# Attention block over 16 images on one core: all engines' programs written out, VectorE's work between two images in another order, and a new start and end

## The reference

```python
xn = group_norm(x)                      # 32 groups, no scale or bias
q, k, v = split(xn.T @ qkv_w.T + qkv_b)
q, k = relu(q), relu(k + pos_enc)       # 8 heads of 32 channels
z   = 1 / (q . sum_tokens(k) + 1e-6)    # per token and head
out = (q @ (k.T @ v)) * z               # linear attention, per head
y   = x + out @ proj_w.T + proj_b
```

## Time and profile before

| what | value |
|---|---|
| median of 3 runs | 2903.65 us (2902.27 to 2904.47) |
| the profiled execution's own time | 2910.53 us |
| its span | 2908.7 us |
| mean granted TensorE clock | 0.993 |
| busy: PE, DVE, ACT, POOL | 94%, 73%, 60%, 53% of the span |

### The profile page before, as it was taken

The page is one execution under the profiler, slowest core; times in us unless marked ns, Lnnn a source line. Parts: engine busy times, 40 slices in busy tenths (PEclk is TensorE's granted clock), DMA queues, the critical chain, the costliest instruction groups (busy, mean ns, idle before and its releaser), DMA issues.

```text
span 2908.7 us, 50163 instructions
## 1 busy us (share of the span) xinstructions
PE 2727.0 (94%) x16232; PEld 2303.3 (79%) x16232; DVE 2115.0 (73%) x2857; ACT 1756.5 (60%) x2565; POOL 1550.9 (53%) x998
## 2 busy tenths in 40 slices
PE   3889999999999999999999999999999999999997
PEld 2767878888787887878888787888878888787875
DVE  6667777777777777777776777777777777777765
ACT  2556656566565666656566665656656566665652
POOL 1435655555464555645555465555646555464544
PEclk9999999999999999999999999999999999999998
DMA  7555656566564665656466574665657466575655
GB/s 233 188 175 171 203 170 207 156 216 196 170 210 155 215 192 181 200 167 208 155 217 196 171 216 158 210 189 184 204 164 215 143 224 189 174 218 160 207 167 166
DMA packets 298173, 548.18 MB, mean 188 GB/s; under 512 B 21216, under 2 KB 41056, under 8 KB 297952
## 3 DMA queue, kind: packets, MB, share of 16 engines
q1 hardware_dynamic: 297952, 545.28, 59.9%
HBM read 433.79 MB, written 111.41 MB: 187 GB/s over the span
## 4 chain that ended last, share of the span: by engine, by line
PE 70%; issue 10%; DVE 9%; ACT 6%; POOL 3%; DMA 2%; SPq 1%; DVEq 0%; ACTq 0%; POOLq 0%
PE psX L482 15%; PE psK L420 15%; PE psX L442 14%; PE psG L432 10%; PE psG L434 5%; PE psT L411 5%; PE psX L458 3%; PE psX L468 2%; DVE kt L716 2%; ACT kt L937 2%; DVE kk L721 1%; DVE q L736 1%; DVE zt L773 1%; POOL kacc L1072 1%; POOL hl L1058 1%
## 5 line engine op out<-in xcount | busy, mean ns | idle before, releaser
L1058 POOL TENSOR_TENSOR hl<-xn,hl 128x512 fp32r<-128x512 f32 x386 | 502.8, 1325 | 676.2 <-ACT hl L926 676.2
L1072 POOL TENSOR_TENSOR kacc<-kacc,kt 128x512 f32<-128x512 f32 x368 | 535.9, 1456 | 544.0 <-ACT kt L937 544.0
L721 DVE TENSOR_TENSOR kk<-kt,kk 128x512 fp32r<-128x512 f32 x400 | 495.9, 1240 | 285.2 <-ACT kk L940 285.2
L420 PE MATMUL psK<-wqk,hl 128*128 128x256 f32 x4608 | 649.3, 291 | 17.1 <-DVE kt L716 11.9
L432 PE MATMUL psG<-kk,xt 128*128 128x512 f32 x1600 | 588.2, 401 | 30.4 <-DVE kk L721 30.1
L420 PEld LDWEIGHTS psK<-wqk,hl 128*128 128x128 f32 x4608 | 579.0, 192 | 26.6 <-issue 17.4
L442 PE MATMUL psX<-hl,wqk 128*128 128x512 f32 x2304 | 599.5, 395 | 0.0
L937 ACT ACTIVATE kt<-kt 128x512 f32<-128x512 f32 x400 | 252.9, 632 | 526.4 <-DVE kt L716 519.0
L482 PE MATMUL psX<-uhl,mhl 128*128 128x512 f32 (+1 forms) x2400 | 563.8, 384 | 7.1 <-POOL uhl L1076 6.2
L482 PEld LDWEIGHTS psX<-uhl,mhl 128*128 128x128 f32 x2400 | 440.1, 189 | 100.6 <-POOL uhl L1076 8.8
L442 PEld LDWEIGHTS psX<-hl,wqk 128*128 128x128 f32 x2304 | 407.2, 188 | 90.2
(11 more groups left out here) (88 smaller groups left out, 2547.6 us busy)
## 6 DMA issues: line engine op xcount, KB each, us to landing
xs<-in_x SPq DMA_DIRECT2D x198, 512.0 KB, 3.9
xa<-in_x SPq DMA_DIRECT2D x195, 512.0 KB, 4.8
xr<-in_x SPq DMA_DIRECT2D x192, 512.0 KB, 3.7
y<-xr SPq DMA_DIRECT2D x192, 512.0 KB, 5.0
posb<-pos_plus_bk SPq DMA_DIRECT2D x377, 256.0 KB, 2.9
posb<-in_pos SPq DMA_DIRECT2D x25, 256.0 KB, 2.8
pos_plus_bk<-posb SPq DMA_DIRECT2D x25, 256.0 KB, 3.7
q<-in_x SPq DMA_DIRECT2D x12, 512.0 KB, 5.6
```

Source lines behind the costliest of these rows:

```text
L420: last = mm(psK[:, i * C:(i + 1) * C], hl_of(t)[:, a, c, s:s + P], wqk[:, w, c, C:2 * C], start=(j == 0), stop=(j == len(terms) - 1))
L721: v.tensor_tensor(kk[:, hp, :, 1, :], kt[:, hp, :].rearrange("p (i n) -> p i n", i=TILES), kk[:, hp, :, 0, :], ALU.subtract).then_inc(kl_r ...
L1058: g.tensor_tensor(hl_of(t)[:, 1, :, s], xn[:, t % 2, :, s], hl_of(t)[:, 0, :, s], ALU.subtract).then_inc(xl_ready, 1)
L1072: g.tensor_tensor(both, both, kt[:, h % 2, :], ALU.add).then_inc(ks_done, 1)
```

## The change

1. All engines' programs are written out for the 16 batches. What the loops did for a 17th batch is gone.
2. Start: all of x is loaded ahead of the constants, with gavg alone after the fourth block. wqk's parts are made by ScalarE and GpSimd. The other constants are loaded behind the first blocks of batch 0 and prepared in its steps 2 to 7. In batch 0 GpSimd adds the key bias to the position blocks (`pos_add`).
3. Junction: `key_scale` is one multiplication, ahead of the copy of ksc; `m_low` moves from the end of step 1 to behind the first `key_add` of step 2; the second group's `invert` is done in halves, in steps 3 and 4, and its `z_mixed` in step 5; the statistics leave steps 1 and 3, and steps 7 and 10 take two blocks.
4. End: `finish` uses the banks of psT, psK and psG too, z and outputs have two pairs of banks each in turn, z runs three blocks ahead, and the key sums come before the output. The last batch's residual x goes into seven places (xs, xa and xr), loaded from batch 15 on.

The diff, cut to its core:

```diff
-        psT = ps("psT", [P, BLK])
-        psK = ps("psK", [P, BLK])
+        psTK = ps("psTK", [P, 2, BLK])
+        psT, psK = psTK[:, 0], psTK[:, 1]
...
+        def last_of(t):
+            if t == LAST:
+                return xs_tail[:]
+            return (xs[:, 0], xs[:, 1], xa[:, 0], xa[:, 1], xr[:, 0], xr[:, 1], xr[:, 2])[t % 7]
...
-                return [(1, s) for s in plan[t]] if t < 9 else [(2, t - 9)]
-            return [(n + 1, t + 4)] if t < 9 else [(n + 2, t - 9)]
+            else:
+                plan = ((5,), (), (6,), (), (7,), (8,), (9,), (10, 11), (12,))
+            ahead = ((0,), (1, 2), (3,), (4,))
+            found = [(n + 1, s) for s in plan[t]] if t < 9 else [(n + 2, s) for s in ahead[t - 9]]
+            return [(sn, s) for sn, s in found if sn < B]
...
+            early = [(wqk_raw, wqk_d.rearrange("c p n -> p c n")), (ident[:], ident_d), (bq[:], bq_d)]
+            late = [(wv[:], wv_d.rearrange("c p n -> p c n")), (pw[:], pw_d.rearrange("c p n -> p c n")), (bmask, bmask_d),
+                    (hmask[:], hmask_d), (bv[:], bv_d), (pb[:], pb_d),
+                    (esel_raw, esel_d.rearrange("p (g c) n -> p g c n", c=CC)[:, :, 0, :])]
...
+            def load_last(t):
+                s = last_slot(t)
+                if t in (4, 5, 6):
+                    sp.wait_ge(y_stored[t - 4], landed3(B - 2, t + 5))
+                elif 7 <= t < LAST:
+                    sp.wait_ge(y_last[s], last_no(t) - 16)
+                sp.dma_start(last_of(t), x_part(B - 1, t)).then_inc(x_last[s], 16)
...
-                    for dst, src in smalls:
-                        sp.dma_start(dst, src).then_inc(w_loaded, 16)
-                    for i in range(TILES):
-                        sp.dma_start(bk_b[:, i, :], bk_d.partition_broadcast(P)).then_inc(w_loaded, 16)
+                    sp.dma_start(gavg[:], gavg_d).then_inc(g_loaded, 16)
+            for dst, src in early:
+                sp.dma_start(dst, src).then_inc(w_loaded, 16)
+            for i in range(TILES):
+                sp.dma_start(bk_b[:, i, :], bk_d.partition_broadcast(P)).then_inc(w_loaded, 16)
             for t in range(2):
                 load_xa(0, t)
                 load_pos(0, t)
+            for dst, src in late:
+                sp.dma_start(dst, src).then_inc(late_loaded, 16)
+            for t in range(2):
                 load_xs(1, t)
             next_xa(0, 0)
-            batch(0)
-            sp.wait_ge(setup_done, 1)
-            batch(1)
-            with sp.Fori(2, B - 2) as n:
+            for n in range(B):
+                if n == 1:
+                    sp.wait_ge(setup_done, 1)
+                    sp.wait_ge(w_low, 1)
...
+                if first(n) and t == 6:
+                    bias_product()
...
             def finish(n):
                 u = [uhl, hl[:, 1], hl[:, 2]]
+                query_a(n, 0)
                 gram(n - 1, NHB - 1)
-                query_a(n, 0)
+                pe.wait_ge(kt_ready, NHB * n)
+                key_sums(n - 1, psK)
                 out_step(n, 0, uhl)
                 z_step(n, 0)
-                key_sums(n - 1)
+                denominators(n - 1, 0, psT)
                 query_b(n, 0)
-                kv_product(n - 1)
-                pe.wait_ge(u_ready, blk_no(n - 2, LAST))
-                denominators(n - 1, 0, 2)
-                pe.wait_ge(zt_ready, 2 * n - 1)
+                kv_product(n - 1, psK)
                 query_a(n, 1)
                 out_step(n, 1, uhl)
-                m_product(n - 1)
+                m_product(n - 1, psK)
                 query_b(n, 1)
-                pe.wait_ge(m_sum, n)
-                denominators(n - 1, 1, 1)
-                pe.wait_ge(q_saved, two_no(n - 1, LAST, 1))
-                spread_z(n - 1, 0)
-                pe.wait_ge(u_ready, blk_no(n - 1, 0))
-                spread_z(n - 1, 1)
+                denominators(n - 1, 1, psG[:, 0])
+                def z_last(t):
+                    if t == 0:
+                        pe.wait_ge(q_saved, two_no(n - 1, LAST, 0))
+                    elif t == 1:
+                        pe.wait_ge(m_sum, n)
+                        pe.wait_ge(zt_ready, 2 * n - 1)
+                    else:
+                        pe.wait_ge(u_ready, blk_no(n - 1, t - 2))
+                    spread_z(n - 1, t, psTK if t % 2 else psX[:, 2:4])
+                for t in range(3):
+                    z_last(t)
                 for t in range(NBLK):
                     def bank_free(m):
-                        if t == 0 and m == 1:
+                        if t == 0 and m == 0:
+                            pe.wait_ge(q_saved, two_no(n - 1, LAST, 1))
+                        elif t == 0:
+                            pe.wait_ge(out_ready, two_no(n - 2, LAST - 1, 1))
+                        elif t == 1:
                             pe.wait_ge(zt_ready, 2 * n)
-                        elif t:
-                            pe.wait_ge(out_ready, two_no(n - 1, t, m) - CC)
-                    output(n - 1, t, u[t % 3], (0, 1), bank_free)
-                    if t + 2 < NBLK:
-                        pe.wait_ge(u_ready, blk_no(n - 1, t + 1))
-                        spread_z(n - 1, t + 2)
-            pe.wait_ge(bvm_ready, 1)
-            for c in range(CC):
-                last = mm(psX[:, 0, c * C:(c + 1) * C], bvm[:, c, :], pw[:, c, :], start=True, stop=True)
-            last.then_inc(bpb_done, 1)
+                        else:
+                            pe.wait_ge(out_ready, two_no(n - 1, t - 2, m))
+                    output(n - 1, t, u[t % 3], psG if t % 2 else psX[:, 0:2], bank_free)
+                    if t + 3 < NBLK:
+                        z_last(t + 3)
...
-                    both = posb[:, s, :].rearrange("p (i n) -> p i n", i=TILES)
-                    v.tensor_tensor(both, both, bk_b[:], ALU.add).then_inc(pos_added, 1)
                     dve.wait_ge(pos_added, h + 1)
...
-                v.tensor_copy(ksc[:], psX[:, 1, 0:CC]).then_inc(ksc_ready, 1)
-                dve.wait_ge(ksc_ready, n + 1)
-                for c in range(CC):
-                    for d in (WIN, WIN + 16):
-                        last = v.tensor_scalar(swin[:, c, d:d + HPC], hmask[:], ksc[:, c:c + 1], None, ALU.mult)
-                last.then_inc(swin_ready, 1)
-            def kv_masked(n):
+                places = swin[:, :, WIN:WIN + 32].rearrange("p c (d r) -> p c d r", d=2)[:, :, :, 0:HPC]
+                v.tensor_tensor(places, hmask[:].unsqueeze(1).unsqueeze(1).broadcast_to([P, CC, 2, HPC]),
+                                bank[:, 0:CC].unsqueeze(2).unsqueeze(3).broadcast_to([P, CC, 2, HPC]),
+                                ALU.mult).then_inc(swin_ready, 1)
+                v.tensor_copy(ksc[:], bank[:, 0:CC]).then_inc(ksc_ready, 1)
...
+                if t == 2 and not first(n):
+                    m_low(n - 1)
...
-                    invert(n - 1, 1)
+                    scale_q(*z_of(n, t), psX[:, 2:4])
+                if t in (3, 4) and not first(n):
+                    invert(n - 1, 1, (t - 3,))
...
-                    m_low(n - 1)
-                    for sn, s in stats_at(n, t):
-                        block_stats(sn, s)
-                if t == 3 and not first(n):
+                    m_total(n - 1, psX[:, 1])
+                if t == 5 and not first(n):
...
-                    residual(n - 1, t)
-                    if t + 2 < NBLK:
-                        scale_q(n - 1, t + 2)
+                    residual(n - 1, t, psG if t % 2 else psX[:, 0:2])
+                    if t + 3 < NBLK:
+                        scale_q(n - 1, t + 3, z_banks(t + 3))
+                    if t < 2:
+                        invert(n - 1, 1, (t,))
+                    if t == 3:
+                        z_mixed(n - 1, 1)
...
+            def pos_add(h):
+                s = pos_slot(h)
+                pool.wait_ge(pos_landed[s], pos_no(0, h))
+                both = posb[:, s, :].rearrange("p (i n) -> p i n", i=TILES)
+                g.tensor_tensor(both, both, bk_b[:], ALU.add).then_inc(pos_added, 1)
...
+            pool.wait_ge(w_high, 1)
+            g.tensor_tensor(wqk[:, 1, :, :], wqk_raw, wqk[:, 0, :, :], ALU.subtract).then_inc(w_low, 1)
+            pos_add(0)
+            pos_add(1)
             xn_low(0, 0)
-            batch(0)
-            batch(1)
-            with pool.Fori(2, B) as n:
+            for n in range(B):
                 batch(n)
             u = [uhl, hl[:, 1], hl[:, 2]]
```

More of the change, by code:

```diff
@@ L249, in has_q @@
         def has_q(n, t):
-            return not (isinstance(n, int) and n == 0 and t < 2)
+            return n > 0 or t >= 2
         def stats_at(n, t):
@@ L603, in batch, with bias_product @@
                     step(n, t)
+            def bias_product():
+                pe.wait_ge(bvm_ready, 1)
+                for c in range(CC):
+                    last = mm(psX[:, 2, c * C:(c + 1) * C], bvm[:, c, :], pw[:, c, :], start=True, stop=True)
```

(59 more changed lines are left out.)

263 lines of the change are left out of this document (127 added, 136 removed).

## The result

| | before | after |
|---|---|---|
| median, same chip | 2902.96 us (4 runs, 2895.62 to 2904.47) | 2816.73 us (4 runs, 2816.62 to 2818.06) |
| ratio after / before, 95% interval | | 0.9709 (0.9692 to 0.9726) |
| profiled execution, its span | 2910.53, 2908.7 us | 2818.06, 2816.3 us |

A forecast was written before the change was run, and what follows sets the result against it. TensorE's work and the places where it stands bound the kernel. Batches -45, start -16, batch 0 0, end -20 and -4 sum to -85: span 2908.7 to 2824, median 2819 us, range 2804 to 2842.

The forecast's parts named there:

- The branches: Loops over batches 2 to 15: ScalarE's taken branch costs it 3.9 us; writing it out saves TensorE 21 us.
- The junction: VectorE's work inside each batch: key sums, M's low part with statistics, and reciprocal, moved or split to close TensorE's holes.
- (a): Key sums' four operations become one: hole of 0.83 us before denominators closes, -12; batch 1's like pair, -2.
- (b): M's low part and statistics leave step 1: 1.31 us hole closes, about 1.1 opens before first output; -5 (0 to -20).
- rival 3: Junction closes entirely: M's low part in time, both reciprocal halves hide; -14 and -20 more, 2785 to 2805 us; chance 0.07.
- (c): Reciprocal of 3.36 us in halves: holes 0.75 and 0.92 become two of about 0.65 us; -5 (+5 to -25).
- (d): Statistics move to steps 7 and 10, and position blocks come sooner: nothing gained or lost.
- The start: x loaded first: statistics by 21.5, first K product 8.5 us later at 30.0 instead of 46.11; -16 (-13 to -18).
- Batch 0: Position sums go to GpSimd, but SP's store and load cycle stays at 11.3 to 11.8 us: 0 (-5 to +12).
- Rival 1: Batch 0 is paced by GpSimd: 12 steps grow by 2.7 us, +32, 2851 us; chance 0.11.
- The end: Last batch: second banks and three blocks under way give outputs 3.2 us apart, -20; first output 4 us earlier, -4.
- Rival 2: The end keeps its pace of 4.2 us a block: 12 us more, 2831 us; chance 0.09.

The follow-up runs named there:

- the experiment with the old statistics: Changed kernel with `m_low` at the end of step 1 and the old plan of the statistics, step 1's behind it: 2824.64 us, ratio 0.9732, period 170.96.
- four places: Changed kernel with four places for position blocks instead of two, in batch 0 alone: 2811.72 us, ratio 0.9689.

## Why the prediction held, step by step

**The branches** (-21): right in cause and size, 17.5 us by medians and 20.3 us of waits; 1.7 us went into longer waits before the denominators.

**The junction** (-24). (a) -12 and -2: measured 14.3. (b) -5: the experiment with the old statistics gives 7.9. The trade of the spread's hole for one before the first output was right; it is 0.79 and not 1.1 us. The step put the old hole down to the subtraction and the statistics together; the runs show that taking the statistics away is enough to close it. What rival 3 calls M's low part in time comes with that part at the end of step 1, as in the kernel before, and not with the change's new place for it. (c) -5: measured 11.8 by medians and 0.76 x 15 = 11.4 by periods. With the whole reciprocal the holes are 0.74 and 0.93 us, as in the earlier trace rows. The two new ones came where they were named, at 0.53 and 0.58 instead of 0.65 us: 0.56 of the 0.76; the other 0.2 us are TensorE's busy time beside the holes, which the step did not count. So -5 was half of what came. (d) 0 as a part of its own: the statistics' gain is in (b). By periods the four experiments give 1.4 + 0.97 + 0.52 + 0.76 = 3.65 us a batch (0.52 is the old statistics' 170.96 less 170.44), and the period fell by 3.66: the four parts add up. Over batches 1 to 15 it is -56.1 where -45 was forecast. This is where the kernel beat the forecast, most of it in (c).

**The start** (-16): the term that failed, by 4.7 us. x came as computed (0.6 us later). The step took over the 8.5 us from statistics to the first product, although it had itself put ScalarE's copy of wqk and GpSimd's subtraction and sums into them. It checked that GpSimd would be free in time, and not what its work does to VectorE's chain of small operations, nor that a copy ahead of the square root leaves the wrong table. The Trainium skill (SBUF — State Buffer, two separate sides) says that VectorE and GpSimd exclude each other for a whole instruction when VectorE's has two SBUF inputs and GpSimd's reads SBUF, or when VectorE's is in a mode that uses both of its ports. The trace agrees for the products of two SBUF inputs, 2.11 us up to the end of GpSimd's instruction where 0.16 is usual; in which mode the one with a single input (1.19 us) ran, no row shows.

**Batch 0** (0): -1.2, and within what this account varies anyhow, so the time tests the step only roughly. VectorE's low parts of the keys, which the step feared for (up to +17), took 1.02 us on average in batch 0, and 1.09 before. Rival 1, the pace of GpSimd, did not come as a loss, but half of its mechanism is there: GpSimd stood 39.4 us for position loads, and TensorE waited 8.6 us in all for low parts of xn behind them. It is SP's cycle that makes it, as four places show, so the step's reading of the earlier trace rows was right.

**The end** (-20 - 4): -19.7 - 4.1, right in both sizes. Outputs came 3.2 us apart at full clock, as computed: from the first to the last 39.7 us pass (2771.38 to 2811.06) for 40.6, and 58.3 passed before (2844.11 to 2902.42). The 67.7 us and the clock of 0.83 that the prediction reads from the earlier trace rows begin 3.1 us ahead of the first output; from 2844.10 on it is 64.6 us at 0.84. Its -20 does not hang on that, as it is worked out from the pairs of the earlier trace rows. Six of them took 58.3 us and not 60.6, which makes 18.6 us; the other 1.0 is behind the last output's start, 5.2 us instead of 6.3. Ahead of the first output the account went from 30.4 to 26.3 us: up to the first spread TensorE's idle time fell from 4.7 to 1.0 us (windows 2813.70 to 2838.50 and 2745.10 to 2765.80), as the step's reasons have it; no run tests them one by one. From that spread to the output it is 5.6 us in both, the last 2.8 of them with TensorE idle. Rival 2 did not come.

**The sum.** The misses, +4.7 for the start, -11.1 for the batches, -1.2 for batch 0 and +0.2 for the end, leave the profiled span 7.4 us under the 2823.7 forecast. That the median is only 2.3 us under its forecast is in part luck: the start's miss took back some of what the batches gave more, and there is a second reason: the step from the profile to the median took off 0.2%, as before, and the changed kernel's median is 0.05% under its profiled execution (2818.06).

## What to carry to other kernels

An operation that moves to another place is priced by what is waiting on its engine at that moment: M's low part, 1.3 us ahead of a save of q, opened a hole of 0.14 us, and statistics of 1.3 us behind it 1.2 us a batch more. A long operation that nobody needs soon (a reciprocal of 3.4 us) belongs in pieces that fit between two handovers; halves gave a third of what quarters gave. And when new work is put beside a chain of tiny dependent operations, the chain's own durations must be forecast anew, not taken over.

## What the runs showed of the hardware

- A taken branch cost ScalarE 3.9 us and TensorE, behind it, about 1.4 us a batch; straight code of 16 batches on four engines showed no such stop.
- A VectorE operation on 128x2 elements took 0.14 to 0.17 us alone and 0.69 to 2.11 us beside a GpSimd operation of 1.24 or 2.34 us, up to that one's end.
- A copy and then a square root on ScalarE needed a table load of 1.28 us between them; a square root and then a copy did not.
- Batch 0, with loads, stores and GpSimd's sums in one cycle, took between 157.7 and 165.7 us to its first key sums in eight profiles of like code with two places, while the changed kernel's later periods, away from the end, lie between 170.43 and 170.57 us.
